# A transformer block on one core: next tile's scores moved one iteration ahead, second norm in other banks, a new order on four engines

## The chip, the cores and the metric

The kernel runs on 1 core of a Trainium2 chip. The metric is the device time of one launch in microseconds: the median of the runs, with their lowest and highest. One execution more is profiled; its rows are the ones read here.

## The reference

128 sequences of 64 tokens and 256 channels go through one transformer block, whose norms take their gain and shift from a condition vector of 64 numbers for each sequence. Everything is float32.

```python
def rmsnorm(x, t, gw, gb, bw, bb):           # gain and shift of each sequence
    g, b = (t @ gw.T + gb)[:, None, :], (t @ bw.T + bb)[:, None, :]
    return g * x * rsqrt(mean(x * x, -1) + 1e-6) + b
def attention(x):                             # 16 heads of 16 channels, 64 x 64 scores
    q, k, v = x @ Wq.T, x @ Wk.T, x @ Wv.T
    return (softmax(q k^T / 4) v) @ Wo.T
def swiglu(x):                                # 1024 hidden channels
    return (silu(x @ gate_w.T) * (x @ hid_w.T)) @ out_w.T
x1  = x + attention(rmsnorm(x, cond, 1))
out = x + x1 + swiglu(rmsnorm(x1, cond, 2))
```

## The kernel before

**Tiles.** A tile is 8 sequences, 512 tokens; there are 16. `iteration(t)` on each engine does the attention of tile t (`attend`), the feed-forward part of tile t-1 (`mlp`; in its names u = t-1), the result of tile t-2 (`finish`) and the first norm and the projections of tile t+1 (`ahead`). Iteration 0 has its own order (`first_tile`), iteration 15 too (`last_tile`); 1 to 14 have the common one, of which 2 to 14 are a loop; 16 and 17 are the common order with parts left out.

**Engines.** Each engine has its own queue, written out by hand in its block, and does it strictly in that order; semaphores join the engines. So a wait at the head of a queue holds up all that stands behind it. TensorE (from L1034) multiplies and transposes into the 8 banks of PSUM: GATE (0), HIDDEN (1), Y and Y+1 (the feed-forward sum), and PAIR to PAIR+3 (attention). ACT (L368), DVE (L674) and GpSimd (L222, written POOL in the rows) work on what comes out. SP (L186) only starts the loads of x and the stores; its order is not touched.

**Precision.** A product of float32 accuracy is made from three passes over operands split in a high and a low part: ACT rounds the high part (`high_norm1`, `high_norm2`, `high_hidden`, `high_attention`, `high_weights`), and GpSimd or DVE subtracts it to have the low part (`low_norm1`, `low_hidden`, `low_weights` on GpSimd; `low_attention` on DVE; of `low_norm2` one channel half on each). Scores, probabilities by values and the transposes are plain float32 products.

**Feed-forward part.** Eight chunks j of 128 hidden channels: `gate(u, j)` and `hid(u, j)`, six products each of 512 columns; ACT `tanh` (L444), DVE `silu` (L786) and `hidden` (L793), ACT `high_hidden` (L449), GpSimd `low_hidden` (L251), then `down(u, j)`, twelve products (L1038 to L1040). `gate(j)` waits for silu(j-1), `hid(j)` for hidden(j-1), since each has one bank.

**Attention.** Two rounds of four pairs of heads. `scores(t, r)` (L1115) fills the four banks PAIR to PAIR+3; for each pair DVE has `row_maxima` (L744) and `shift` (L751), ACT `exp` (L454), DVE `reciprocals` (L758, L763), GpSimd `divide` (L257), TensorE `transpose_probs` (L1123), ACT `keep_transposed` (L459); then `values_probs` (L1139), ACT `first_heads` (L465), DVE `second_heads` (L769), and the high and low part for `project_out`. `scores(t, 1)` waits for second_heads of round 0.

**Norms.** ACT `mean_squares` (L389), GpSimd `inverse_rms` (L231, L234), scaling of the rows (`scale_rows`, DVE L681, four instructions, for the first norm; `scale_second`, ACT L494, and `scale_second_rest`, DVE L688, for the second), eight transposes (`transpose_norm1` L1045, `transpose_norm2` L1054), gain and shift (`first_norm1/2` on DVE, L699 and L706; `second_norm1/2` on ACT, L399, eight instructions), high part (L413, L418), low part (GpSimd L239, L245; DVE L719). The first norm's transposes write GATE and HIDDEN and therefore wait until hidden(5) of the feed-forward part is done (`h_done` 8u+6). The second norm's write PAIR+2 and PAIR+3. `first_residual` (L846) adds the attention to x, `results` (L802) makes the output, `sum_of_inputs` (L280) prepares it. In iteration 0 the splits of the last two weights are made between the pieces of the softmax (`low_weights`, L264).

Of the kernel before, what the change touches and what calls it, by code (L numbers as in the profile page):

```python
# [27 lines left out]
P = 128  # L28
# [25 lines left out]
def conditioned_block(nc, x, condT, modT, attW, gateT, hidT, outT, consts, out):  # L54
# [3 lines left out]
    with ExitStack() as ctx:  # L58
# [164 lines left out]
        def _(pool):  # L223
# [58 lines left out]
            def first_tile(t, attend, mlp, finish, ahead):  # L282
                divide(t, 0)
                inverse_rms(t + 1, ms1, ms1_done, mse1, mse1_done, inv1, inv1_done, scaled1)
# [17 lines left out]
            def last_tile(t, attend, mlp, finish, ahead):  # L302
                sum_of_inputs(t - 1)
                low_hidden(t - 1, 0)
                low_hidden(t - 1, 1)
                divide(t, 0)
                divide(t, 1)
                divide(t, 2)
                divide(t, 3)
                low_hidden(t - 1, 2)  # L310
                low_hidden(t - 1, 3)
                divide(t, 4)
                divide(t, 5)
                low_hidden(t - 1, 4)
                divide(t, 6)
                divide(t, 7)
                low_hidden(t - 1, 5)
                wait(pool, scaled2_rest, t)
                inverse_rms(t, ms2, ms2_done, mse2, mse2_done, inv2, inv2_done, scaled2)
                low_hidden(t - 1, 6)  # L320
                low_hidden(t - 1, 7)
                low_norm2(t)

            def iteration(t, attend, mlp, finish, ahead):
# [10 lines left out]
                if mlp:  # L335
                    low_hidden(t - 1, 1)
                    low_hidden(t - 1, 2)
                if attend:
                    divide(t, 2)
                    divide(t, 3)  # L340
                if mlp:
                    low_hidden(t - 1, 3)
                if ahead:
                    inverse_rms(t + 1, ms1, ms1_done, mse1, mse1_done, inv1, inv1_done, scaled1)
                    low_norm1(t + 1, 0)
                    low_norm1(t + 1, 1)
                if attend:
                    divide(t, 4)
                if mlp:
                    low_hidden(t - 1, 4)  # L350
# [18 lines left out]
        def _(act):  # L369
# [37 lines left out]
            def second_norm2(u):  # L407
                second_norm(u, 2, ps[:, PAIR + 3, :], xT2_done, (xn2_lo_second, u), xn2, xn2_second)
# [94 lines left out]
            def first_tile(t, attend, mlp, finish, ahead):  # L503
                keep_input(t)
                mean_squares(1, x_in, x_loaded, (32, 32), x_scaled1, xT1_done, ms1, ms1_done)
# [3 lines left out]
                exp(t, 2)  # L509
                keep_transposed(t, 1)  # L510
                exp(t, 3)
                high_norm1(t + 1, 0)
                high_weights(2, hid_w_in, 16, hid_w_hi[:, :, :].rearrange("p c n -> p (c n)"), 0)
                keep_transposed(t, 2)
                keep_transposed(t, 3)
                high_weights(3, out_w_in, 16, out_w_hi[:, :, :].rearrange("p j n -> p (j n)"), 1)
                first_heads(t, 0)
                exp(t, 4)
                high_attention(t, 0)
                second_norm1(t + 1, GATE + 1)  # L520
                high_norm1(t + 1, 1)
# [3 lines left out]
                exp(t, 7)  # L525
                keep_transposed(t, 5)
                first_keys(t + 1)
# [7 lines left out]
                first_queries(t + 1)  # L535
# [4 lines left out]
            def last_tile(t, attend, mlp, finish, ahead):  # L540
                tanh(t - 1, 0)
                tanh(t - 1, 1)
                high_hidden(t - 1, 0)
                exp(t, 0)
                keep_input(t)
                exp(t, 1)
                high_hidden(t - 1, 1)
                tanh(t - 1, 2)
                exp(t, 2)
                tanh(t - 1, 3)  # L550
                high_hidden(t - 1, 2)
                keep_transposed(t, 0)
                exp(t, 3)
                keep_transposed(t, 1)
                tanh(t - 1, 4)
                high_hidden(t - 1, 3)
                keep_transposed(t, 2)
                keep_transposed(t, 3)
                first_heads(t, 0)
                exp(t, 4)  # L560
                tanh(t - 1, 5)
                high_hidden(t - 1, 4)
                exp(t, 5)
                exp(t, 6)
                tanh(t - 1, 6)
                exp(t, 7)
                high_attention(t, 0)
                high_hidden(t - 1, 5)
                keep_transposed(t, 4)
                keep_transposed(t, 5)  # L570
                keep_transposed(t, 6)
                keep_transposed(t, 7)
# [4 lines left out]
                high_hidden(t - 1, 6)  # L577
                scale_second(t)
                high_hidden(t - 1, 7)
                high_norm2(t, 0)  # L580
                second_norm2(t)
                high_norm2(t, 1)

            def iteration(t, attend, mlp, finish, ahead):
                if isinstance(t, int) and t == 0:
                    return first_tile(t, attend, mlp, finish, ahead)
                if isinstance(t, int) and t == TILES - 1:
                    return last_tile(t, attend, mlp, finish, ahead)
                if mlp:
                    tanh(t - 1, 0)  # L590
                if attend:
                    exp(t, 0)
                if mlp:
                    high_hidden(t - 1, 0)
                    tanh(t - 1, 1)
                if attend:
                    exp(t, 1)
                    keep_input(t)
                if mlp:
                    tanh(t - 1, 2)  # L600
                if attend:
                    exp(t, 2)
                if mlp:
                    high_hidden(t - 1, 1)
                if attend:
                    keep_transposed(t, 0)
                if mlp:
# [839 lines left out]
```

## Time and profile before

| | us |
|---|---|
| median of 3 runs | 1004.91 |
| lowest and highest | 1001.57, 1005.65 |
| the profiled execution | 1001.78 |
| its span, first to last instruction | 999.8 |
| TensorE busy | 958.1 |
| DVE, ACT, GpSimd busy | 660.1, 561.7, 447.4 |
| mean granted TensorE clock | 0.985 |

The rows of the profile have these forms. A timeline row is: start in us from the span's start, duration, engine, line of the kernel, operation, written tile <- read tiles, shape, how many merged, and in brackets the idle time before it with what ended it. PE is TensorE, PEld its weight loads. Products are pipelined: each row of TensorE is longer than the distance to the next, so the distance between starts is what a product costs (0.23 us for 512 columns), and short waits show only in that distance. Row groups are numbered; the prediction refers to them.

### The profile page before, as it was taken

What the parts mean: (1) busy time and instruction counts of PE and PEld (TensorE: products, weight loads), DVE (VectorE), ACT (ScalarE), POOL (GpSimd) and SP (SyncE); (2) the same over time, 40 slices, a digit from 0 to 9 for tenths busy, and PEclk for the clock granted to TensorE, in tenths of its full rate; (3) what the DMA queues carried; (4) which work ended last, traced back from release to release, by engine and by line L of the source; (5) the groups of instructions that cost most, each with busy time, mean ns of one, the idle gap of its engine ahead of it and who ended that gap; (6) DMA issues with size and microseconds to landing.
All of it is one profiled execution on the core that took longest, in us unless ns stands there. A gap on an engine that the chain in (4) does not pass through costs nothing.

```text
span 999.8 us, 24465 instructions
## 1 busy us (share of the span) xinstructions
PE 958.1 (96%) x9134; PEld 819.7 (82%) x9134; DVE 660.1 (66%) x1178; ACT 561.7 (56%) x1271; POOL 447.4 (45%) x393
## 2 busy tenths in 40 slices
PE   6678999999999999999999999999999999999978
PEld 5467888988888897888889788888978888897767
DVE  3546767676776767677676767767676776766642
ACT  4445656565565656556565655656565565654442
POOL 4443525454452545445254544525454452545242
PEclk9868999999999999999999999999999999999999
DMA  5100000010100001010000101000010100000000
GB/s 168 58 1 22 2 23 22 2 42 0 42 0 21 21 0 42 0 42 0 21 21 0 42 0 42 0 21 21 0 42 0 42 0 21 21 0 22 2 22 22
DMA packets 18971, 21.71 MB, mean 22 GB/s; under 512 B 640, under 2 KB 18240, under 8 KB 18816
## 3 DMA queue, kind: packets, MB, share of 16 engines
q1 hardware_dynamic: 18720, 21.24, 6.4%
q8 instruction: 18, 0.29, 0.1%
q10 hardware_dynamic: 224, 0.10, 0.1%
q14 instruction: 9, 0.07, 0.0%
HBM read 12.95 MB, written 8.39 MB: 21 GB/s over the span
## 4 chain that ended last, share of the span: by engine, by line
PE 89%; ACT 3%; DVE 3%; POOL 2%; issue 2%; DMA 1%; DVEq 0%; ACTq 0%; POOLq 0%
PE ps L1038 10%; PE ps L1040 9%; PE ps L1039 9%; PE ps L1115 6%; PE ps L1150 6%; PE ps L1166 6%; PE ps L1123 6%; PE ps L1158 5%; PE ps L1169 5%; PE ps L1151 5%; PE ps L1167 5%; PE ps L1139 3%; PE ps L1062 3%; PE ps L1065 3%; PE ps L1063 3%
## 5 line engine op out<-in xcount | busy, mean ns | idle before, releaser
L251 POOL TENSOR_TENSOR h_lo<-h,h_hi 128x512 fp32r<-128x512 f32 x128 | 165.2, 1291 | 248.3 <-ACT h_hi L449 248.3
L257 POOL TENSOR_TENSOR probs<-probs,recip 128x512 f32<-128x512 f32 x128 | 132.4, 1045 | 50.5 <-DVE recip L763 50.5
L1038 PE MATMUL ps<-out_w_hi,h_hi 128*128 128x256 f32 x512 | 150.8, 294 | 0.8
L1040 PE MATMUL ps<-out_w_hi,h_lo 128*128 128x256 f32 x512 | 145.0, 283 | 0.0
L1039 PE MATMUL ps<-out_w_lo,h_hi 128*128 128x256 f32 x512 | 144.7, 283 | 0.0
L786 DVE SCALAR_TENSOR_TENSOR shared<-shared,ps 128x512 f32<-128x512 f32 x128 | 87.7, 685 | 77.9 <-ACT shared L444 77.5
L444 ACT ACTIVATE shared<-ps 128x512 f32<-128x512 f32 x128 | 76.7, 600 | 101.5 <-PE ps L1158 100.1
L1150 PE MATMUL ps<-xn_hi,gate_w_hi 128*128 128x512 f32 x256 | 109.5, 428 | 2.3 <-ACT xn_hi L418 1.6
L1166 PE MATMUL ps<-xn_hi,hid_w_hi 128*128 128x512 f32 x256 | 106.1, 414 | 0.9 <-DVE h L793 0.9
L1038 PEld LDWEIGHTS ps<-out_w_hi,h_hi 128*128 128x128 f32 x512 | 97.0, 190 | 11.6 <-POOL h_lo L251 7.2
L459 ACT COPY probsT<-ps 128x512 f32<-128x512 f32 x128 | 73.5, 588 | 50.9 <-PE ps L1123 50.2
L1151 PE MATMUL ps<-xn_hi,gate_w_lo 128*128 128x512 f32 x256 | 101.2, 395 | 0.0
L1167 PE MATMUL ps<-xn_hi,hid_w_lo 128*128 128x512 f32 x256 | 101.0, 395 | 0.0
L793 DVE SCALAR_TENSOR_TENSOR h<-shared,ps 128x512 f32<-128x512 f32 x128 | 87.4, 683 | 18.2 <-PE ps L1169 13.1
L1039 PEld LDWEIGHTS ps<-out_w_lo,h_hi 128*128 128x128 f32 x512 | 97.0, 190 | 1.4
L1040 PEld LDWEIGHTS ps<-out_w_hi,h_lo 128*128 128x128 f32 x512 | 96.8, 189 | 0.0
L744 DVE TENSOR_REDUCE row_max<-ps 128x8 f32<-128x512 f32 x128 | 84.7, 681 | 16.1 <-PE ps L1115 16.1
L449 ACT CAST h_hi<-h 128x512 fp32r<-128x512 f32 x128 | 79.2, 619 | 27.9 <-DVE h L793 27.9
L454 ACT ACTIVATE probs<-probs 128x512 f32<-128x512 f32 x128 | 79.5, 637 | 26.7 <-DVE probs L751 26.7
L758 DVE TENSOR_REDUCE sums<-probs 128x8 f32<-128x512 f32 x128 | 86.2, 673 | 11.9 <-ACT probs L454 11.8
L239 POOL TENSOR_TENSOR xn_lo<-xn,xn_hi 128x512 fp32r<-128x512 f32 x30 | 38.4, 1301 | 117.7 <-ACT xn_hi L413 117.7
L751 DVE TENSOR_TENSOR probs<-ps,row_max 128x512 f32<-128x512 f32 x128 | 87.5, 684 | 1.9
(92 smaller groups left out, 2155.7 us busy)
## 6 DMA issues: line engine op xcount, KB each, us to landing
x_in<-in_x SPq DMA_DIRECT2D x16, 512.0 KB, 3.4
out<-result SPq DMA_DIRECT2D x15, 512.0 KB, 3.0
shared<-in_attT SPq DMA_DIRECT2D x1, 1024.0 KB, 7.5
shared<-in_gateT SPq DMA_DIRECT2D x1, 1024.0 KB, 9.4
shared<-in_hidT SPq DMA_DIRECT2D x1, 1024.0 KB, 4.8
shared<-in_outT SPq DMA_DIRECT2D x1, 1024.0 KB, 5.6
out<-result SPq DMA_DIRECT2D x2, 256.0 KB, 2.2
result<-in_modT SPq DMA_DIRECT2D x1, 256.0 KB, 4.7
```

Source lines behind the costliest of these rows:

```text
L251: nc.gpsimd.tensor_tensor(h_lo[:, j % KEPT, :], h[:, j % 2, :], h_hi[:, j % KEPT, :].bitcast(F32), ALU.subtract).then_inc(h_lo_done, 1)
L257: nc.gpsimd.tensor_tensor(own, own, recip[:, p % TOGETHER, :].unsqueeze(2).to_broadcast([P, SEQS, L]), ALU.mult).then_inc(divided, 1)
L751: nc.vector.tensor_tensor(probs[:, p % TOGETHER, :].rearrange("p (b k) -> p b k", k=L), ps[:, bank_of(p), :].rearrange("p (b k) -> p b k", ...
L786: nc.vector.scalar_tensor_tensor(act_g[:, :], act_g[:, :], 1.0, ps[:, GATE, :], ALU.add, ALU.mult).then_inc(silu_done, 1)
L793: nc.vector.scalar_tensor_tensor(h[:, j % 2, :], act_g[:, :], 0.5, ps[:, HIDDEN, :], ALU.mult, ALU.mult).then_inc(h_done, 1)
L1038: nc.tensor.matmul(dst, a_hi, b_hi, start=first, stop=False, skip_group_check=skip)
L1039: nc.tensor.matmul(dst, a_hi, b_lo, start=False, stop=False, skip_group_check=skip)
L1040: return nc.tensor.matmul(dst, a_lo, b_hi, start=False, stop=last, skip_group_check=skip)
L1150: nc.tensor.matmul(ps[:, GATE, :], gate_w_hi[:, i, w], xn2_hi[:, i, :], start=i == 0, stop=False)
L1151: nc.tensor.matmul(ps[:, GATE, :], gate_w_lo[:, i, w], xn2_hi[:, i, :], start=False, stop=False)
L1166: nc.tensor.matmul(ps[:, HIDDEN, :], hid_w_hi[:, i, w], xn2_hi[:, i, :], start=i == 0, stop=False)
L1167: nc.tensor.matmul(ps[:, HIDDEN, :], hid_w_lo[:, i, w], xn2_hi[:, i, :], start=False, stop=False)
```

## The change

The instructions are the same in kind and number; they are put in another order on TensorE, ACT, DVE and GpSimd, and two banks are changed.

- `scores(t+1, 0)` is issued at the end of iteration t, ahead of the transposes of the second norm, and no longer at the head of iteration t+1. It waits for `first_residual` of tile t (the banks PAIR+2, PAIR+3) and not for the second norm. DVE takes `row_maxima(t+1, 0)` and `shift(t+1, 0)` into iteration t. The scores of tile 0 stand in front of iteration 0.
- `transpose_norm2` writes GATE and HIDDEN (banks 0 and 1), and so waits for all eight hidden chunks of the tile before.
- All four orders are written anew: for the first tile, the last, and the common one.

The diff, cut to the norm, the waits, and the common order of each engine:

```diff
             def second_norm2(u):                                   # ACT
-                second_norm(u, 2, ps[:, PAIR + 3, :], xT2_done, (xn2_lo_second, u), xn2, xn2_second)
+                second_norm(u, 2, ps[:, HIDDEN, :], xT2_done, (xn2_lo_second, u), xn2, xn2_second)
...
             def transpose_norm2(u, c):                             # TensorE
                 pe.wait_ge(scaled2, u + 1)
                 pe.wait_ge(scaled2_rest, u + 1)
-                pe.wait_ge(x1_done, 2 * u + 2)
+                wait(pe, h_done, CHUNKS * u)
...
-                    last = nc.tensor.transpose(ps[:, PAIR + 2 + c, k * P:(k + 1) * P],
+                    last = nc.tensor.transpose(ps[:, GATE + c, k * P:(k + 1) * P],
...
             def scores(t, r):
...
-                    wait(pe, gained2, t)
-                    wait(pe, xn2_second, t)
+                    wait(pe, x1_done, 2 * t)
```

The common order after the change, from the new lines of the diff, conditions left out (t is the tile of attention, u = t-1 of the feed-forward part, n = t+1). What stands in brackets was the order before in the same stretch.

```
GpSimd: low_hidden(u,0) sum_of_inputs(u) divide(t,0) divide(t,1) low_hidden(u,1) divide(t,2)
        low_hidden(u,2) divide(t,3) low_hidden(u,3) inverse_rms(n) low_hidden(u,4) divide(t,4)
        low_norm1(n,0) low_norm1(n,1) divide(t,5) divide(t,6) divide(t,7) low_hidden(u,5) ...
        [... low_hidden(u,3) inverse_rms(n) low_norm1(n,0) low_norm1(n,1) divide(t,4)
        low_hidden(u,4) divide(t,5) ...]
ACT:    exp(t,0) tanh(u,0) exp(t,1) high_hidden(u,0) tanh(u,1) high_hidden(u,1) exp(t,2) tanh(u,2)
        keep_input(t) keep_transposed(t,0) tanh(u,3) high_hidden(u,2) exp(t,3) mean_squares(n)
        tanh(u,4) keep_transposed(t,1) high_hidden(u,3) keep_transposed(t,2) keep_transposed(t,3)
        first_heads(t,0) tanh(u,5) high_hidden(u,4) high_attention(t,0) exp(t,4) second_norm1(n)
        high_norm1(n,0) tanh(u,6) high_norm1(n,1) exp(t,5) keep_transposed(t,4) exp(t,6) exp(t,7)
        high_hidden(u,5) first_keys(n) keep_transposed(t,5) keep_transposed(t,6) first_queries(n)
        keep_transposed(t,7) first_heads(t,1) first_values(n) high_attention(t,1) high_hidden(u,6)
        mean_squares(t) tanh(u,7) scale_second(t) high_hidden(u,7) second_norm2(t) high_norm2(t)
        [... keep_transposed(t,3) tanh(u,5) high_hidden(u,4) first_heads(t,0) second_norm1(n) ...]
DVE:    row_maxima(t,1) low_norm2(u) shift(t,1) results(t-2) silu(u,0) hidden(u,0) row_maxima(t,2)
        row_maxima(t,3) reciprocals(t,0) shift(t,2) silu(u,1) hidden(u,1) reciprocals(t,1)
        silu(u,2) hidden(u,2) reciprocals(t,2) shift(t,3) silu(u,3) hidden(u,3) reciprocals(t,3)
        silu(u,4) hidden(u,4) second_heads(t,0) scale_rows(n) silu(u,5) hidden(u,5)
        row_maxima(t,4) row_maxima(t,5) shift(t,4) first_norm1(n) reciprocals(t,4) ...
        second_heads(t,1) low_attention(t,1) second_queries(n) second_values(n) first_residual(t)
        silu(u,7) hidden(u,7) scale_second_rest(t) row_maxima(n,0) first_norm2(t) shift(n,0)
        [results(t-2) low_norm2(u) row_maxima(t,0) row_maxima(t,1) shift(t,0) silu(u,0) ...
        hidden(u,4) silu(u,5) second_heads(t,0) scale_rows(n) hidden(u,5) row_maxima(t,4)
        row_maxima(t,5) first_norm1(n) shift(t,4) ...]
TensorE: gate hid (u,0) gate hid (u,1) down(u,0) gate hid (u,2) transpose_probs(t,0) gate hid (u,3)
        transpose_probs(t,1) gate hid (u,4) transpose_probs(t,2) transpose_probs(t,3) gate(u,5)
        values_probs(t,0) hid(u,5) scores(t,1) transpose_norm1(n) down(u,1) down(u,2) gate(u,6)
        down(u,3) transpose_probs(t,4) hid(u,6) project_k(n,0) transpose_probs(t,5) project_q(n,0)
        transpose_probs(t,6) project_k(n,1) transpose_probs(t,7) project_v(n,0) values_probs(t,1)
        project_q(n,1) project_v(n,1) down(u,4) project_out(t) gate(u,7) hid(u,7) scores(n,0)
        transpose_norm2(t) down(u,5) down(u,6) down(u,7)
        [scores(t,0) gate hid (u,0) ... transpose_norm1(n) down(u,1) gate(u,6) hid(u,6) down(u,2)
        down(u,3) ... values_probs(t,1) down(u,4) gate(u,7) project_k(n,1) project_out(t)
        project_v(n,1) hid(u,7) down(u,5) transpose_norm2(t) down(u,6) down(u,7)]
```

Of the first tile's order this matters here:

```diff
             def first_tile(t, attend, mlp, finish, ahead):        # GpSimd
...
-                low_weights(3, out_w_lo[:, :, :].rearrange("p j n -> p (j n)"),
-                            out_w_hi[:, :, :].rearrange("p j n -> p (j n)"), 1)
                 low_norm1(t + 1, 0)
+                low_norm1(t + 1, 1)
                 divide(t, 4)
-                low_norm1(t + 1, 1)
                 divide(t, 5)
                 divide(t, 6)
                 divide(t, 7)
+                low_weights(3, out_w_lo[:, :, :].rearrange("p j n -> p (j n)"),
+                            out_w_hi[:, :, :].rearrange("p j n -> p (j n)"), 1)
```

In the same tile ACT does `high_weights(2, ...)` ahead of `mean_squares(1, ...)` instead of behind exp(3). In the last tile GpSimd does low_hidden(14, 6) ahead of the second norm's inverse_rms instead of behind it, ACT does second_norm2 ahead of both high_norm2, and TensorE does gate(14, 7) ahead of the transposes of pairs 5 to 7, hid(14, 7) and project_out(15) directly behind values_probs(15, 1), and down(14, 4) and down(14, 5) behind project_out(15).

## Rows read from the trace of the kernel before

**Rows 1.** The page's busy table: engine, busy us (share of the span), instructions.
```profile
PE 958.1 (96%) x9134; PEld 819.7 (82%) x9134; DVE 660.1 (66%) x1178; ACT 561.7 (56%) x1271; POOL 447.4 (45%) x393
```

**Rows 2.** What TensorE waited for: us in total, times, longest us.
```profile
PE ps L1123 <- POOL probs L257: 10.8, 5, 4.8
...
PE ps L1054 <- ACT shared L494: 4.4, 2, 3.5
...
PE ps L1115 <- ACT shared L399: 2.7, 1, 2.7
```

**Rows 3.** Busy us by engine in two stretches; then granted clock, DMA share, GB/s.
```profile
core 0: us, PE busy (x) PEld busy (x) DVE busy (x) ACT busy (x) POOL busy (x), PEclk, DMA share, GB/s
492.00:551.00 59.00, 58.92 (x585) 50.62 (x586) 40.95 (x74) 35.25 (x82) 26.91 (x24) 1.00 0.06 18
...
900.00:955.00 55.00, 47.59 (x492) 39.62 (x490) 36.70 (x62) 24.72 (x50) 22.42 (x20) 0.98 0.03 11
```

**Rows 4.** Timeline of TensorE, one middle iteration: start us, us, engine, line, operation, tiles.
```profile
492.38 2.02 PE L1115 MATMUL ps<-keys,queries 32*128 32x64 f32 x64
...
502.00 0.39 PE L1150 MATMUL ps<-xn_hi,gate_w_hi 128*128 128x512 f32 x1
...
503.40 0.39 PE L1166 MATMUL ps<-xn_hi,hid_w_hi 128*128 128x512 f32 x1
...
550.61 2.01 PE L1115 MATMUL ps<-keys,queries 32*128 32x64 f32 x64
```

**Rows 5.** Timeline around the end of that iteration, four engines.
```profile
546.75 1.06 PE L1054 MATMUL ps<-consts_sb,shared 128*128 128x128 f32 x8
...
550.32 1.17 ACT L418 CAST xn_hi<-shared 128x512 fp32r<-128x512 f32 x2
...
550.80 1.29 DVE L802 TENSOR_TENSOR result<-ps,x_plus_x 128x512 f32<-128x512 f32 x2 [1.75 <-PE ps L1040]
...
551.05 1.27 POOL L245 TENSOR_TENSOR xn_lo<-shared,xn_hi 128x512 fp32r<-128x512 f32 x1 [2.63 <-ACT xn_hi L418]
...
552.01 0.87 DVE L719 TENSOR_TENSOR xn_lo<-shared,xn_hi 128x512 fp32r<-128x512 f32 x1
...
552.56 0.50 PE L1150 MATMUL ps<-xn_hi,gate_w_hi 128*128 128x512 f32 x1
...
555.62 0.50 PE L1150 MATMUL ps<-xn_hi,gate_w_hi 128*128 128x512 f32 x1
```

**Rows 6.** Timeline between the two rounds of the next iteration, three engines.
```profile
572.08 0.60 ACT L444 ACTIVATE shared<-ps 128x512 f32<-128x512 f32 x1 [0.81 <-PE ps L1158]
...
572.57 0.61 ACT L449 CAST h_hi<-h 128x512 fp32r<-128x512 f32 x1
...
573.18 0.69 ACT L465 ACTIVATE attT_sum<-ps,consts_sb 128x512 f32<-128x512 f32 x1
...
573.90 0.75 DVE L769 SCALAR_TENSOR_TENSOR attT_sum<-ps,consts_sb,attT_sum 128x512 f32<-128x512 f32 x1 [0.51 <-ACT attT_sum L465]
...
574.57 1.13 DVE L681 TENSOR_SCALAR x_scaled<-x_in,inv 128x256 f32<-128x256 f32 x4
...
574.71 2.01 PE L1115 MATMUL ps<-keys,queries 32*128 32x64 f32 x64
...
575.62 0.68 DVE L793 SCALAR_TENSOR_TENSOR h<-shared,ps 128x512 f32<-128x512 f32 x1
...
576.65 1.09 PE L1045 MATMUL ps<-consts_sb,x_scaled 128*128 128x128 f32 x8
```

**Rows 7.** Timeline of DVE's row scaling beside GpSimd, first and last tile.
```profile
36.05 1.04 POOL L257 TENSOR_TENSOR probs<-probs,recip 128x512 f32<-128x512 f32 x1
...
36.11 1.91 DVE L681 TENSOR_SCALAR x_scaled<-x_in,inv 128x256 f32<-128x256 f32 x4 [0.23 <-POOL inv L234]
...
951.57 1.26 POOL L251 TENSOR_TENSOR h_lo<-h,h_hi 128x512 fp32r<-128x512 f32 x1
...
951.63 1.61 DVE L688 TENSOR_SCALAR shared<-shared,inv 128x256 f32<-128x256 f32 x2 [2.42 <-POOL inv L234]
```

**Rows 8.** Timeline of GpSimd in the first tile.
```profile
49.46 4.51 POOL L264 TENSOR_TENSOR out_w_lo<-shared,out_w_hi 128x2048 fp32r<-128x2048 f32 x1
```

More of the change, by code:

```diff
@@ L344, in iteration @@
                     inverse_rms(t + 1, ms1, ms1_done, mse1, mse1_done, inv1, inv1_done, scaled1)
+                if mlp:
+                    low_hidden(t - 1, 4)
+                if attend:
+                    divide(t, 4)
+                if ahead:
                     low_norm1(t + 1, 0)
                     low_norm1(t + 1, 1)
[L347 to L350, printed above, removed]
                 if attend:
@@ L595, in iteration @@
                     tanh(t - 1, 1)
+                    high_hidden(t - 1, 1)
                 if attend:
-                    exp(t, 1)
-                    keep_input(t)
+                    exp(t, 2)
                 if mlp:
@@ L601, in iteration @@
                 if attend:
[L602 to L605, printed above, removed]
+                    keep_input(t)
                     keep_transposed(t, 0)
                 if mlp:
+                    tanh(t - 1, 3)
                     high_hidden(t - 1, 2)
-                    tanh(t - 1, 3)
                 if attend:
@@ L626, in iteration @@
                 if attend:
-                    first_heads(t, 0)
+                    high_attention(t, 0)
+                    exp(t, 4)
                 if ahead:
@@ L827, in _ @@
             second_values(0)
+            row_maxima(0, 0)
+            shift(0, 0)
             def maxima_and_shift(t, p):
@@ L948, in iteration @@
                 if attend:
-                    row_maxima(t, 0)
-                    row_maxima(t, 1)
-                    shift(t, 0)
+                    shift(t, 1)
+                if finish:
+                    results(t - 2)
                 if mlp:
@@ L955, in iteration @@
                 if attend:
-                    shift(t, 1)
+                    row_maxima(t, 2)
+                    row_maxima(t, 3)
                     reciprocals(t, 0)
+                    shift(t, 2)
                 if mlp:
                     silu(t - 1, 1)
+                    hidden(t - 1, 1)
                 if attend:
@@ L1029, in iteration @@
                     scale_second_rest(t)
+                if ahead:
+                    row_maxima(t + 1, 0)
+                if attend:
                     first_norm2(t)
+                if ahead:
+                    shift(t + 1, 0)
             over_tiles(dve, iteration)
@@ L1214, in _ @@
                 project_v(0, half)
+            scores(0, 0)
             def project_out(t):
@@ L1291, in last_tile @@
                 hid(u, 6)
-                down(u, 2)
+                down(u, 3)
+                if ahead:
+                    pe.wait_ge(q_act_done, t + 2)
+                gate(u, 7)
                 transpose_probs(t, 5)
-                down(u, 3)
                 transpose_probs(t, 6)
@@ L1299, in last_tile @@
                 if ahead:
-                    pe.wait_ge(q_act_done, t + 2)
-                gate(u, 7)
+                    pe.wait_ge(q_dve_done, t + 2)
+                hid(u, 7)
+                project_out(t)
                 down(u, 4)
                 down(u, 5)
-                project_out(t)
-                if ahead:
-                    pe.wait_ge(q_dve_done, t + 2)
-                hid(u, 7)
                 for c in range(CH):
@@ L1403, in iteration @@
                     hid(u, 7)
-                    down(u, 5)
+                if ahead:
+                    scores(t + 1, 0)
                 if attend:
```

257 lines of the change are left out of this document (125 added, 132 removed).

## The prediction

> **What bounds the kernel now.** I read the busy table first. TensorE is busy for 958.1 us of a span of 999.8 and no other engine for more than 66% of it, so TensorE bounds the kernel [rows 1]. The list of what TensorE waited for comes next: longest first, three of its twelve entries shown, and none occurs more than five times, so these waits belong to the first and the last tile and not to the middle [rows 2]. In the middle 59 us, TensorE is busy 58.92 at a granted clock of 1.00 [rows 3]. Last the timeline of one middle iteration: scores start at 492.38 and again at 550.61, a period of 58.23 us [rows 4]. Fourteen of the sixteen iterations run this period (t = 1 to 14), so 0.1 us an iteration is 1.4 us of the kernel.
>
> How much of that period could an order give back? A gate or hidden block of six products takes 1.40 us when nothing is in its way (502.00 to 503.40, [rows 4]). With undisturbed lengths read off the same timeline an iteration is 20 such blocks (gate, hidden, queries, keys) of 1.40, 10 of 1.43 (down, values), the output projection 2.84, twice scores 1.94, twice probabilities by values 1.09, and transposes 4.5: 55.7 us. The other 2.5 us are about 0.1 us wherever a block of plain fp32 products hands over to the split ones (0.50 instead of 0.39 for the first product, [rows 4, 5]), which happens 12 times before and 11 times after, 0.1 at the start of each block of scores or of probabilities by values, and waits of 0.1 to 0.2 that the idle column does not show. So the new order can save at most about 0.9 us an iteration, 12 us in all. What it can lose has no such limit: each wait of TensorE in the loop is paid 14 times.
>
> **The loop, part by part.** No product, activation or transfer is added or dropped, so only borders and waits count.
>
> *Scores one iteration early, second norm into the gate banks.* Before, scores and two down blocks stand between the second norm's transposes (546.75) and the gate (552.56), and the transposes wait for the scaled rows. After, gate, hidden and the scores stand behind the output projection, which is 0.4 us more cover for first residual, mean square, power and scaling, so the transposes no longer wait. The gate follows down(7) directly. Behind the transposes come three down blocks, 0.82 + 1.5 + 1.44 + 1.44 = 5.2 us. xn2_hi is complete 4.74 us after the transposes start (550.32 + 1.17 - 546.75, [rows 5]): ready with 0.4 to spare. Together with one hand-over less and small waits gone before hid(6), Tn2 and the seventh probability transpose I count -0.5 us (bounds -0.9 and 0).
>
> *DVE at the start of an iteration.* results (1.29 us, [rows 5]) used to run under the scores, ahead of low_norm2. Now down(7) ends only when the gate begins, and the queue reads row_maxima(1), low_norm2, shift(1), results, silu(0). low_norm2 ends at 5.2 + 0.9 behind the start of the transposes if it must wait for the GpSimd instruction, which it does (below); shift adds 0.6, results 1.25, silu 0.65: gate start + 3.4. gate(1) needs that silu and is ready at gate start + 2.8; it used to start 3.06 after its predecessor (552.56 to 555.62). That is +0.4 of which 0.2 comes back, because down(0) then no longer waits for h_lo: +0.2. The last two products of gate(0) need the low part at +0.93 and get it at about +0.95: +0.1. Bounds for both together 0 and +0.5.
>
> *The step that decides: hidden(5) and the first norm of the next tile.* TensorE may transpose the next tile's rows into GATE and HIDDEN only after hidden(5) (h_done 8u+6). Before, tanh(5) ran at 572.08, silu(5) at 572.71, then second_heads, scale_rows, hidden(5) at 575.62 to 576.30, and the transposes began at 576.65 without waiting [rows 6]. Now ACT does first_heads before tanh(5), and DVE does second_heads, scale_rows, silu(5), hidden(5). Let F be the start of first_heads (573.18 before; it follows the probabilities by values, so it doesn't move). second_heads is F+0.72 to F+1.47, scale_rows F+1.39 to F+2.52 [rows 6]. silu(5) then ends at F+3.15 and hidden(5) at F+3.85. Scores(1) start at F+1.53 and last 1.94, so TensorE is ready at F+3.47: a wait of 0.4 us, new, even if nothing else happens.
>
> *But something else stands there now.* low_hidden(4), 1.29 us on GpSimd, is moved from behind both low_norm1 to directly behind inverse_rms. It waits only for high_hidden(4), which ACT does right behind tanh(5). ACT instructions of this size follow each other every 0.5 us (572.08, 572.57, [rows 6]), so high_hidden(4) ends at F+1.7 and GpSimd starts at F+1.8, in the middle of the four instructions of scale_rows. Twice the trace shows this DVE instruction against a GpSimd one. At 36.11 the four take 1.91 us instead of 1.13, under a GpSimd instruction that ends at 37.09; at 951.63 two take 1.61 instead of half of 1.13, under one that ends at 952.83 [rows 7]. Everywhere else in the loop GpSimd is idle under scale_rows, and there it is 1.13. low_norm2 behaves likewise (at 552.01, 0.87 us and done 0.56 after the GpSimd instruction that began at 551.05, [rows 5]). So DVE loses the rest of the GpSimd instruction. One or two of the four are through when it arrives; the others start about F+3.3 and end at F+3.7; silu(5) ends F+4.35, hidden(5) F+5.05, and the transposes start at F+5.1 instead of F+3.47: a wait of 1.6 us, where the 0.4 stood. Bounds: 0.4 (DVE keeps its place through all four, GpSimd waits) and 1.9 (GpSimd gets in after the first). No row shows a GpSimd instruction that arrives in the middle of such a group, so this is my choice: the two rows say that the one that comes later waits, instruction by instruction. I take 1.6.
>
> The Trainium skill (SBUF — State Buffer, Who interferes with whom) says that DVE instructions such as tensor_scalar in their two-port mode share one port pair with GpSimd, and that the first to issue holds it "for the whole instruction". The two rows agree in size. It speaks of one instruction, so by the rule GpSimd gets in between two of the four and the iteration loses the 1.6; read as a hold over the whole group it would lose 0.4. The same page says that tensor_reduce never contends, and the row maxima and sums would then be free of this in the new order too.
>
> *The rest of the iteration* has to be walked for waits that follow. first_norm1, shift(4), exp(4) and second_norm1 all start behind hidden(5), so they shift with the transposes; xn1_lo is complete about 8.2 us behind them and project_k needs it after down(1), down(2), gate(6), down(3), one transpose and hid(6), 8.6 us. Attention's low part is ready 1.3 us before the output projection. keep_input moves 1.4 us later on ACT, its load lands 3.4 us after issue and mean_squares still finds it. Cost 0, with +0.3 as the upper bound, since three of these margins are under 0.4.
>
> Loop: -0.5 + 0.3 + 1.6 = +1.4 us an iteration, 14 times +19.6 us.
>
> **First tile.** The split of out_w (4.51 us on GpSimd at 49.46) stood before divide(4), and the transposes of probabilities waited 4.8 us for what came behind it ([rows 8] and the first line of [rows 2]). It moves behind divide(7). high_weights(2) moves to where ACT waits for the load of x. divide(4) then follows exp(4), about 3 us earlier. The scores of tile 1 move out from behind the second norm, where TensorE waited 2.7 us and ran them at the lower clock ([rows 2], third line); in their place it waits for the norm uncovered, 4.7 us after the transposes. Net about -1. Sum -4; bounds -7.5 (both waits gone whole) and 0.
>
> **Last tile.** scale_second_rest no longer meets low_hidden(6) (951.63, 1.0 us too long, [rows 7]), and second_norm2 is put before high_norm2(0), but project_out now stands right behind hid(7), with less between it and the last round. -1; bounds -3.5 (the wait for x_scaled2, second line of [rows 2]) and +2.
>
> **Sum.** +19.6 - 4 - 1 = +14.6 us. The profiled execution took 1001.78 us (span 999.8 and 2.0 around it), so 1016.4 by its own time; the median of the three runs shown lies 3.1 us above it, which puts the changed kernel's median at 1019.5; I say 1019. A difference under 0.5%, 5 us, is what I call the same.
>
> **Rivals.** (a) *No collision:* GpSimd comes a little later or waits. Then 0.4 instead of 1.6, loop +0.2, 14 x 0.2 - 5 = -2: 1003. For it: nothing in the trace shows an arrival in mid-group. Against: the two instants hang on the same event F and lie 0.7 us inside the group. Chance 0.17. (b) *The order does what it can:* hidden(5) and silu(0) are both in time, and the small savings hold: -0.5 x 14 - 5 = -12: 993. For it: TensorE's list shows no wait in the loop now, so the queues have slack. Against: it needs SBUF work and first_heads shorter by 0.4 us than they have been in all 15 tiles. Chance 0.17. (c) *The scores change nothing* since TensorE is full anyway; that is contained in (a). (d) *Clock:* 1.6 us of waiting each iteration lowers the granted clock and all that follows runs slower, over 1030. Against: the last tile's stretch of 55 us has 7.4 us without TensorE work in it and a mean clock of 0.98 ([rows 3], second line). Chance 0.05. The forecast (collision, +1.0 to +1.8 an iteration) has 0.61; its own range is 1010 to 1027.
>
> The range takes in (a): 1001 to 1027. Faster 0.18, same 0.17, slower 0.65.
>
> **What would show it.** In the changed profile: TensorE's list has a wait for DVE's h (L793) before the first norm's transposes, 14 times, 1.3 to 1.7 us each; scale_rows lasts 2.3 us instead of 1.13 with low_hidden inside it; period 59.6; gate(1) starts 3.4 us behind gate(0); no wait before the second norm's transposes; divide(4) of tile 0 near 53. If scale_rows stays at 1.13 and the period is near 58.4, the collision was wrong and the rest stands. If the period is under 58, the placement of first_heads was harmless and I misread the chain behind F.

## The result, and the profile after

The changed kernel takes 1028.79 us (median of four runs, 1027.54 to 1029.90), the kernel before 1003.71 in the same comparison (1001.57 to 1005.65). The ratio is 1.025, interval 1.0223 to 1.0277: 25 us slower. The forecast was 1019, slower, between 1001 and 1027. The direction came true; the time lies 10 us above the forecast and 2 us outside the range. The profiled execution took 1028.87 us, with a span of 1026.8 (before: 999.8).

The page of the changed kernel: busy time of each engine, the granted clock of TensorE in 40 slices, and the chain of work that ended last, by engine. The first line answers to [rows 1].

```profile
PE 964.8 (94%) x9134; PEld 827.9 (81%) x9134; DVE 684.9 (67%) x1178; ACT 561.4 (55%) x1271; POOL 456.9 (44%) x393
...
PEclk9989999999999999999999999999999999999999
...
PE 82%; DVE 10%; issue 3%; ACT 2%; POOL 1%; DMA 1%; DVEq 0%; SPq 0%; ACTq 0%; POOLq 0%
```

TensorE is busy 6.7 us longer than before, yet no product was added; the span grew by 27.0. The slices of 25 us hide the clock: all read 9 in the middle, although the mean granted clock of the execution fell from 0.985 to 0.973.

What TensorE waited for (total us, times, longest), to be held against [rows 2]:

```profile
PE ps L1046 <- DVE h L796: 20.1, 14, 1.4
PE ps L1125 <- POOL probs L257: 9.4, 5, 5.0
...
PE ps L1152 <- ACT xn_hi L421: 4.5, 2, 3.7
...
PE ps L1152 <- DVE shared L789: 2.9, 14, 0.3
```

Before, no wait occurred more than five times. Now the first norm's transposes (L1046) wait for DVE's product h 14 times, 20.1 us in all, once in each full iteration: this is the step on which the forecast rested. The fourth line is gate(1) waiting 0.2 us for silu(0).

The same instant in a middle iteration, after; it answers to [rows 6]. Columns: start, duration, engine, line, operation, and in brackets the idle time before it and what ended that.

```profile
587.54 0.69 ACT L468 ACTIVATE attT_sum<-ps,consts_sb 128x512 f32<-128x512 f32 x1 [1.86 <-PE ps L1141]
588.13 0.59 ACT L447 ACTIVATE shared<-ps 128x512 f32<-128x512 f32 x1
588.26 0.75 DVE L772 SCALAR_TENSOR_TENSOR attT_sum<-ps,consts_sb,attT_sum 128x512 f32<-128x512 f32 x1 [3.25 <-ACT attT_sum L468]
588.60 0.62 ACT L452 CAST h_hi<-h 128x512 fp32r<-128x512 f32 x1
588.93 2.15 DVE L684 TENSOR_SCALAR x_scaled<-x_in,inv 128x256 f32<-128x256 f32 x4
589.07 2.01 PE L1117 MATMUL ps<-keys,queries 32*128 32x64 f32 x64
...
589.30 1.36 POOL L251 TENSOR_TENSOR h_lo<-h,h_hi 128x512 fp32r<-128x512 f32 x1 [2.03 <-ACT h_hi L452]
591.00 0.67 DVE L789 SCALAR_TENSOR_TENSOR shared<-shared,ps 128x512 f32<-128x512 f32 x1
591.71 0.69 DVE L796 SCALAR_TENSOR_TENSOR h<-shared,ps 128x512 f32<-128x512 f32 x1
```

With F = 587.54, the start of first_heads: scale_rows starts at F+1.39 as forecast, GpSimd's low_hidden(4) starts at F+1.76 inside it, and the four DVE instructions take 2.15 us where they took 1.13. silu(5) and hidden(5) follow, and TensorE's transposes start at F+4.98 (forecast: F+5.1):

```profile
592.52 1.65 PE L1046 MATMUL ps<-consts_sb,x_scaled 128*128 128x128 f32 x8 [1.44 <-DVE h L796]
```

So far the forecast holds to 0.2 us. What it left out stands in the windows (busy us and instructions of each engine, then the granted clock), of the loop and of three stretches of this iteration:

```profile
100.00:900.00 800.00, 777.08 (x7548) 670.26 (x7547) 560.19 (x965) 452.81 (x1040) 361.52 (x316) 0.98 0.05 17
589.00:592.80 3.80, 2.36 (x68) 2.16 (x68) 3.77 (x8) 0.74 (x2) 1.36 (x1) 1.00 0.00 0
592.80:596.20 3.40, 3.40 (x19) 3.40 (x18) 3.25 (x6) 1.98 (x6) 0.00 (x0) 0.51 0.00 0
596.40:650.00 53.60, 53.38 (x486) 45.51 (x484) 35.25 (x62) 31.40 (x72) 26.18 (x23) 1.00 0.06 20
```

After the wait the granted clock is 0.51 for 3.4 us, 1.2 GHz of 2.4, and then full again ("clock stretch" below). The products show it too: one of the down block takes 0.41 us in that stretch and 0.28 behind it.

```profile
594.40 0.41 PE L1041 MATMUL ps<-out_w_hi,h_lo 128*128 128x256 f32 x1
...
597.04 0.28 PE L1041 MATMUL ps<-out_w_hi,h_lo 128*128 128x256 f32 x1
```

Such a stretch follows the wait in 11 of the 14 iterations (all but t = 2, 7 and 11). Before, the loop had none.

**Where the 27.0 us are.** I cut both executions at the start of the second gate block of iterations 1 and 15. Before:

```profile
89.90 0.40 PE L1150 MATMUL ps<-xn_hi,gate_w_hi 128*128 128x512 f32 x1
...
905.25 0.50 PE L1150 MATMUL ps<-xn_hi,gate_w_hi 128*128 128x512 f32 x1
```

and after:

```profile
85.42 0.47 PE L1152 MATMUL ps<-xn_hi,gate_w_hi 128*128 128x512 f32 x1
...
934.62 0.50 PE L1152 MATMUL ps<-xn_hi,gate_w_hi 128*128 128x512 f32 x1
```

The start is 4.5 us shorter. The 14 periods between take 849.2 instead of 815.35, +33.85 (60.66 each instead of 58.24). The rest, to the end of the span (the tail), takes 92.2 instead of 94.55, -2.35. Sum +27.0. Of the loop, the three iterations without a clock stretch have periods of 59.45 to 59.48, that is +1.22 an iteration or +17 us; the other eleven have about 61.0, 1.5 more each, which is the remaining 17 us.

### The profile page after: what moved, and what is told of

Same layout as the page of the kernel before. It is cut to its first block, busy times and chain, and to the rows that moved or that the text cites. A ratio compares the mean times of both kernels' runs of the same rounds, so it can differ in the third digit from the quotient of the medians.

```text
span 1026.8 us, 24437 instructions
## 1 busy us (share of the span) xinstructions
PE 964.8 (94%) x9134; PEld 827.9 (81%) x9134; DVE 684.9 (67%) x1178; ACT 561.4 (55%) x1271; POOL 456.9 (44%) x393
## 4 chain that ended last, share of the span: by engine, by line
PE 82%; DVE 10%; issue 3%; ACT 2%; POOL 1%; DMA 1%; DVEq 0%; SPq 0%; ACTq 0%; POOLq 0%
PE ps L1039 9%; PE ps L1041 9%; PE ps L1040 9%; PE ps L1152 6%; PE ps L1125 5%; PE ps L1168 5%; PE ps L1160 5%; PE ps L1171 5%; PE ps L1169 5%; PE ps L1153 5%; PE ps L1141 3%; PE ps L1117 3%; PE ps L1065 3%; DVE x_scaled L684 3%; PE ps L1066 3%; PE ps L1068 3%
## 5 line engine op out<-in xcount | busy, mean ns | idle before, releaser
L251 POOL TENSOR_TENSOR h_lo<-h,h_hi 128x512 fp32r<-128x512 f32 x128 | 169.1, 1322 | 241.7 <-ACT h_hi L452 239.8
L257 POOL TENSOR_TENSOR probs<-probs,recip 128x512 f32<-128x512 f32 x128 | 135.0, 1065 | 136.7 <-DVE recip L766 136.7
L1039 PE MATMUL ps<-out_w_hi,h_hi 128*128 128x256 f32 x512 | 154.6, 302 | 0.0
L1041 PE MATMUL ps<-out_w_hi,h_lo 128*128 128x256 f32 x512 | 149.3, 292 | 0.0
L1040 PE MATMUL ps<-out_w_lo,h_hi 128*128 128x256 f32 x512 | 149.2, 291 | 0.0
L1152 PE MATMUL ps<-xn_hi,gate_w_hi 128*128 128x512 f32 x256 | 107.0, 418 | 7.5 <-ACT xn_hi L421 4.5
L1039 PEld LDWEIGHTS ps<-out_w_hi,h_hi 128*128 128x128 f32 x512 | 103.0, 201 | 6.6 <-POOL h_lo L251 5.7
L1040 PEld LDWEIGHTS ps<-out_w_lo,h_hi 128*128 128x128 f32 x512 | 102.4, 200 | 0.8
L1041 PEld LDWEIGHTS ps<-out_w_hi,h_lo 128*128 128x128 f32 x512 | 101.8, 199 | 0.0
L1125 PE MATMUL ps<-consts_sb,probs 128*128 128x128 f32 x512 | 75.2, 275 | 9.5 <-POOL probs L257 9.4
```

Of the source, the lines that this page charges most:

```text
L251: nc.gpsimd.tensor_tensor(h_lo[:, j % KEPT, :], h[:, j % 2, :], h_hi[:, j % KEPT, :].bitcast(F32), ALU.subtract).then_inc(h_lo_done, 1)
L257: nc.gpsimd.tensor_tensor(own, own, recip[:, p % TOGETHER, :].unsqueeze(2).to_broadcast([P, SEQS, L]), ALU.mult).then_inc(divided, 1)
L1039: nc.tensor.matmul(dst, a_hi, b_hi, start=first, stop=False, skip_group_check=skip)
L1040: nc.tensor.matmul(dst, a_hi, b_lo, start=False, stop=False, skip_group_check=skip)
L1041: return nc.tensor.matmul(dst, a_lo, b_hi, start=False, stop=last, skip_group_check=skip)
L1125: last = nc.tensor.transpose(ps[:, bank_of(p), k * P:(k + 1) * P], probs[:, p % TOGETHER, k * P:(k + 1) * P], ident)
```

## The experiments

The theory after the result: the mishap is one wait, made of 0.4 us of order and 1.0 us of collision; it costs itself and, in most iterations, a stretch at half clock that costs as much again. The rivals: the collision is not what makes scale_rows long; the clock falls for another reason than this wait; the moves named in the change cost by themselves. "Period" below is the mean of the 14 periods cut as above; times are medians, and each ratio is against the kernel before on the same chip.

**1. The collision taken away** (GpSimd's queue of the changed kernel):

```
-                if mlp:
-                    low_hidden(t - 1, 4)
                 if attend:
                     divide(t, 4)
                 if ahead:
                     low_norm1(t + 1, 0)
                     low_norm1(t + 1, 1)
+                if mlp:
+                    low_hidden(t - 1, 4)
```

> The changed kernel with one line moved: in the common order GpSimd does low_hidden(4) behind both low_norm1 again, so that it is idle while DVE scales the rows. Theory (collision, then wait, then clock): scale_rows falls from 2.15 to 1.13 us, TensorE's wait before the first norm's transposes from 1.4 to 0.3-0.4, the half-clock stretches of 3.4 us behind that wait (11 of 14 iterations) are gone, the period is near 58.4. Time 1028.8 - 14 x 1.0 - 11 x 1.6 = 997, within 3. Rival (the clock falls because of the new order as a whole, not because of this wait): only the wait shortens, 1028.8 - 14 = 1014. Second rival (first_heads ahead of tanh(5) is what costs, not GpSimd): over 1020.

Measured: 1004.86 us, ratio 1.002 (1.0004 to 1.0036), 24 us less than the changed kernel. Its timeline has scale_rows short and the wait at the forecast remainder of 0.4:

```profile
573.69 1.13 DVE L684 TENSOR_SCALAR x_scaled<-x_in,inv 128x256 f32<-128x256 f32 x4
...
576.27 1.09 PE L1046 MATMUL ps<-consts_sb,x_scaled 128*128 128x128 f32 x8 [0.43 <-DVE h L796]
```

No clock stretch is left in the loop. The time is 8 us above the 997 expected. Most of that is the period, 58.82 and not 58.4: low_hidden(4) now holds up divide(5), so the transposes of probabilities behind the first block of keys wait too (from the start of that block to theirs it is 1.71 us instead of 1.40, and the wait on probs counts 15 times instead of 5). A queue that is relieved at one place is loaded at another. The last tile also has 6.8 us at half clock here, and the tail is 2.8 us longer than that of the changed kernel (95.0).

**2. The wait filled, the collision kept**: six products with zero weights, added into a bank that is being accumulated.

```
                     if mlp:
+                        for n in range(6):
+                            nc.tensor.matmul(ps[:, Y, :], zeros[:, :], att_w_hi[...],
+                                             start=False, stop=False, ...)
                         pe.wait_ge(h_done, CHUNKS * u + 6)
```

> The changed kernel with six more products of 512 columns, weights zero, accumulated into the feed-forward bank behind scores(t,1), where TensorE would wait for hidden(5): 6 x 0.23 = 1.4 us of work in the place of the wait; nothing else changes. Theory: DVE and GpSimd still collide (scale_rows 2.15) and the transposes start no earlier, but TensorE is not idle and its clock stays: period 59.5 in all iterations, 1028.8 - 11 x 1.6 = 1011. Rival (clock drops have nothing to do with the wait): 1029 or a little more.

Measured: 1014.04 us (1010.00 to 1016.35), ratio 1.0122 (1.0084 to 1.0161), 3 us above the expectation. The loop, and DVE's scaling (count, then shortest, median and longest ns of one):

```profile
100.00:900.00 800.00, 797.23 (x7797) 683.26 (x7797) 571.54 (x984) 463.60 (x1058) 369.84 (x322) 1.00 0.05 17
```
```profile
L687 DVE TENSOR_SCALAR x_scaled<-x_in,inv x64: 340/346/1361, 9.9 to 877.6; 128x256 f32<-128x256 f32 x64
```

The collision is there (1361 ns for the instruction that is caught), TensorE is late by the same time, but it is busy instead of waiting: no clock stretch in the loop, and a period of 59.46, the one of the undisturbed iterations of the changed kernel. 14 x (60.66 - 59.46) = 16.8 us is therefore the price of the lowered clock, and idleness ahead of the transposes is what lowers it in this loop.

**3. The chain around F put right, GpSimd's order kept**: ScalarE does tanh(5) and high_hidden(4) before first_heads, VectorE silu(5) before second_heads.

```
-                    first_heads(t, 0)
                 if mlp:
                     tanh(t - 1, 5)
                     high_hidden(t - 1, 4)
                 if attend:
+                    first_heads(t, 0)
                     high_attention(t, 0)
...
                     hidden(t - 1, 4)
+                    silu(t - 1, 5)
...
                     scale_rows(t + 1, x_in, inv1, ...)
                 if mlp:
-                    silu(t - 1, 5)
                     hidden(t - 1, 5)
```

> The changed kernel with two moves in the common order: ACT does tanh(5) and high_hidden(4) ahead of first_heads(0) again, DVE silu(5) ahead of second_heads(0) again; GpSimd's order stays as changed, so low_hidden(4) now starts before scale_rows and is nearly over when that begins. Theory: hidden(5) is done before TensorE has finished scores(1); no wait, no clock drop, period 57.8 to 58.1. Time 1028.8 - 14 x 1.5 - 11 x 1.6 = 990, within 4. Rival (clock falls with the order as a whole): 1028.8 - 20 = 1008.

Measured: 991.94 us (989.21 to 992.28), ratio 0.9891 (0.9866 to 0.9916): 37 us under the changed kernel and 11 under the one before, the best version of all. Its timeline:

```profile
567.18 0.69 DVE L789 SCALAR_TENSOR_TENSOR shared<-shared,ps 128x512 f32<-128x512 f32 x1 [2.15 <-ACT shared L447]
...
567.73 1.30 POOL L251 TENSOR_TENSOR h_lo<-h,h_hi 128x512 fp32r<-128x512 f32 x1 [0.44 <-ACT h_hi L452]
...
569.04 1.13 DVE L684 TENSOR_SCALAR x_scaled<-x_in,inv 128x256 f32<-128x256 f32 x4
...
570.09 0.68 DVE L796 SCALAR_TENSOR_TENSOR h<-shared,ps 128x512 f32<-128x512 f32 x1
571.12 0.53 PEld L1046 LDWEIGHTS ps<-consts_sb,x_scaled 128*128 128x128 f32 x5
```

low_hidden(4) ends at 569.03 and scale_rows begins at 569.04: the two no longer overlap. hidden(5) ends 0.35 us before the transposes, so nothing waits for it. Period 57.96, and 92.2 us of tail.

**4. A longer wait without the collision**: experiment 1 with two reductions of 0.6 us over a constant tile between scale_rows and silu(5).

```
                     scale_rows(t + 1, x_in, inv1, ...)
+                    for n in range(2):
+                        nc.vector.tensor_reduce(unused[:, n, :], att_w_hi[...], AX_X, ALU.max)
```

> The first experiment (low_hidden(4) out of the way) with two DVE reductions of 0.6 us over a constant tile put between scale_rows and silu(5): the wait of TensorE is made again, 0.4 + 1.2 = 1.6 us, but without any meeting of DVE and GpSimd. Theory: scale_rows stays at 1.13, the half-clock stretches come back in most iterations, time 1028 to 1033. Rival (it is the shared access of DVE and GpSimd that slows things, not the length of the wait): 997 to 1014.

Measured: 1041.03 us, ratio 1.0396 (1.0373 to 1.0419), 8 us above the upper end of the expectation.

```profile
596.14 1.13 DVE L685 TENSOR_SCALAR x_scaled<-x_in,inv 128x256 f32<-128x256 f32 x4
597.19 1.27 DVE L988 TENSOR_REDUCE unused<-att_w_hi 128x8 f32<-128x512 f32 x2
...
599.90 0.54 PE L1051 MATMUL ps<-consts_sb,x_scaled 128*128 128x128 f32 x3 [1.61 <-DVE h L797]
```
```profile
600.40:603.80 3.40, 3.40 (x19) 3.40 (x18) 3.22 (x7) 2.20 (x7) 0.00 (x0) 0.51 0.00 0
```

With scale_rows undisturbed the wait of 1.61 us alone lowers the clock, and in all 14 iterations. The period is 61.40: 58.82 of experiment 1, 1.2 more of wait, and 1.4 of clock. I had counted on fewer stretches.

**5. Half that delay** (one reduction):

> The fourth experiment with one DVE reduction of 0.6 us instead of two: a wait of about 1.0 us before the first norm's transposes, without GpSimd. So far 0.4 us left the clock alone, 1.4 lowered it in 11 of 14 iterations, 1.6 in all. If the length of the wait decides and 1.0 is short enough: no half-clock stretch, 1004.9 + 14 x 0.6 = 1013. If any wait near 1 us is enough: all 14, 1035. I expect the first or a few drops, 1013 to 1020.

Measured: 1014.63 us, ratio 1.0114 (1.0082 to 1.0147). The wait is 1.0 us in every iteration; two of the fourteen have a clock stretch (periods 60.9, the others 59.1 to 59.3). Stretches by length of the wait, then: 0.4 us none in 14 (experiment 1), 1.0 two, 1.44 eleven, 1.61 fourteen.

The length does not decide alone. Iterations 2, 7 and 11 of the changed kernel had the same 1.44 us as the others and kept a full clock, and in experiment 4 all periods are alike, so its fourteen say less than fourteen different cases would. The last tile shows it too. In every trace TensorE waits 1.58 us there, ahead of the scores of the second round and not ahead of transposes. The changed kernel has a full clock around it (scores at 955.26), experiment 1 has half the clock for 6.8 us just behind the same wait (scores at 928.47):

```profile
951.00:960.00 9.00, 7.42 (x153) 6.29 (x152) 4.07 (x7) 3.00 (x6) 2.13 (x2) 1.00 0.01 2
...
929.60:936.40 6.80, 6.80 (x51) 6.10 (x48) 4.52 (x8) 1.66 (x3) 1.70 (x2) 0.50 0.01 2
```

Experiments 2, 5 and 6 have 3.4 us at half clock behind this wait, experiments 8 and 9 have 6.8, and the kernel before and experiments 3, 4 and 7 have none. What chooses between them stays open.

**6. Another block as cover**: down(1) goes ahead of the first norm's transposes, as cover for hidden(5).

```
                     scores(t, 1)
+                if mlp:
+                    down(u, 1)
                 if ahead:
...
                 if mlp:
-                    down(u, 1)
                     down(u, 2)
```

> The changed kernel with down(1) issued ahead of the first norm's transposes instead of behind them: 1.44 us of work that was already there goes into the wait of 1.4 us. Theory: the wait for hidden(5) and the clock drops are gone, but the chain from these transposes to the low part of the norm has 1.4 us less in front of project_k, which begins to wait by 0.5 to 1.1 us; period 58.5 to 59.1, time 995 to 1008. Rival (a filled wait is a saved wait): period 58.0, time 991.

Measured: 1006.63 us, ratio 1.0036 (1.0018 to 1.0053). The wait for h is gone and no clock stretch is in the loop, but the block is missing where it stood:

```profile
PE ps L1065 <- POOL xn_lo L239: 9.2, 14, 0.7
```

The keys now wait up to 0.7 us for the norm's low part. Period 59.01. Taking 1.44 us of cover away leaves a wait of 0.66, so the margin ahead of project_k was about 0.8 us, twice the 0.4 that the prediction named.

**7. The named moves alone**: to the kernel before, only the scores ahead, the gate banks for the second norm, down(5) behind its transposes, and VectorE's new head of the iteration.

```
-                if finish:
-                    results(t - 2)
+                if attend:
+                    row_maxima(t, 1)
                 if mlp:
                     low_norm2(t - 1)
...
+                if ahead:
+                    row_maxima(t + 1, 0)
                 if attend:
                     first_norm2(t)
+                if ahead:
+                    shift(t + 1, 0)
...
-                    last = nc.tensor.transpose(ps[:, PAIR + 2 + c, k * P:(k + 1) * P],
+                    last = nc.tensor.transpose(ps[:, GATE + c, k * P:(k + 1) * P],
```

> The kernel before with only the named moves: scores of the next tile ahead of the second norm's transposes, down(5) behind them, these transposes into the GATE and HIDDEN banks, and DVE's first five items of an iteration as the changed kernel has them. ACT's and GpSimd's orders and everything from hidden(0) to the last project_v stay as before. Theory: TensorE was full, so the scores' early start is worth only border effects: period 58.0 to 58.4 where it was 58.24, no clock drop in the loop, time within 5 us of the kernel before (1003). Rival (the moves are what gains, the rest of the new order only loses): 990 to 995. Second rival (the moves themselves bring the loss): over 1010.

Measured: 1007.58 us, ratio 1.0039 (1.0023 to 1.0054). The period is 58.32 against 58.24. What the change is named after is worth nothing in the loop, +0.1. It costs 5.0 us once, at the end of tile 0: the scores no longer stand behind the second norm's transposes, so TensorE waits for the norm uncovered, ahead of the first gate block, which starts 4.5 us later than before (85.14):

```profile
89.62 0.76 PE L1155 MATMUL ps<-xn_hi,gate_w_hi 128*128 128x512 f32 x1 [3.68 <-ACT xn_hi L418]
```

In the last tile its transposes of the second norm wait 4.1 us where they waited 3.5, and the tail stays at 94.6.

**8 and 9. Two tries for more, on top of experiment 3**: results later in VectorE's queue, behind hidden(0),

```
                 if attend:
                     shift(t, 1)
-                if finish:
-                    results(t - 2)
                 if mlp:
                     silu(t - 1, 0)
                     hidden(t - 1, 0)
+                if finish:
+                    results(t - 2)
```

> The third experiment (tanh(5) and silu(5) early, 991.9 us) with results(t-2) put behind hidden(0) on DVE instead of ahead of silu(0). Theory: gate(1) no longer waits 0.2 to 0.3 us for silu(0) in 14 iterations, of which up to 0.2 comes back as down(0)'s wait for h_lo: -0.1 to -0.3 an iteration, 988 to 990. Rival (DVE's order there costs nothing): 992.

and the same with row_maxima(2), row_maxima(3) and shift(2) behind hidden(1) as well.

> The third experiment (991.9 us) with DVE's head of the iteration in the order silu(0), hidden(0), results(t-2), reciprocals(0), silu(1), hidden(1), and row_maxima(2), row_maxima(3), shift(2) behind these. The sixth experiment lost because three softmax items stood between results and silu(1), so that gate(2) waited 0.7 us. Theory: gate(1) begins 0.3 us earlier, down(0) gives 0.2 of it back, gate(2) does not wait; period 57.7 to 57.9, 988 to 990. Rival (the maxima pushed back now delay the softmax and a later step of TensorE): period 58.2 or more, 995.

Both missed. The first took 1004.10 us (ratio 1.0011, 0.9998 to 1.0024), 12 more than experiment 3. In experiment 3 results fills the time before silu(0); now VectorE is idle there for 0.92 us, and results delays all between hidden(0) and silu(1), for which gate(2) waits:

```profile
561.31 0.50 PE L1152 MATMUL ps<-xn_hi,gate_w_hi 128*128 128x512 f32 x1 [0.72 <-DVE shared L789]
```

This wait of 0.7 us comes in nearly every iteration and lowers no clock; the period is 58.81. The second took 996.31 (0.9944, 0.9927 to 0.9961), with a period of 58.14 instead of 57.96: gate(3) now starts 0.25 us later against the block before it, since silu(2) stands behind the softmax items that were pushed back:

```profile
556.28 0.69 DVE L789 SCALAR_TENSOR_TENSOR shared<-shared,ps 128x512 f32<-128x512 f32 x1 [0.35 <-ACT shared L447]
...
557.02 0.19 PEld L1152 LDWEIGHTS ps<-xn_hi,gate_w_hi 128*128 128x128 f32 x1 [0.24 <-DVE shared L789]
```

Each has the 6.8 us at half clock in its last tile, 95.0 us of tail instead of 92.2.

## Why the prediction was right in direction and wrong in size

- **"The step that decides"**: right. It forecast 14 waits of 1.3 to 1.7 us for h; there are 14 of 1.44. Experiments 1 and 3 take the collision away in two different ways and the wait shrinks to 0.43 or goes.
- **"Something else stands there now"**: right in the choice between its bounds. GpSimd does get in between two of the four, as the Trainium skill's rule of one instruction (SBUF — State Buffer, Who interferes with whom) has it; the group takes 2.15 us, where 2.3 was forecast, and the three that are not caught stay at 0.34 to 0.35.
- **-0.5 for borders and small waits, +0.3 for VectorE's head**: their sum, -0.2, is what the undisturbed period leaves: 59.46 - 58.24 - 1.44 = -0.2. The parts were not measured one by one, except that scores, banks and head together give +0.1 in experiment 7. gate(1) starts 3.41 us behind gate(0), forecast 3.4, by these rows of the changed kernel:

```profile
627.85 0.39 PE L1152 MATMUL ps<-xn_hi,gate_w_hi 128*128 128x512 f32 x1
...
631.26 0.50 PE L1152 MATMUL ps<-xn_hi,gate_w_hi 128*128 128x512 f32 x1 [0.20 <-DVE shared L789]
```

- **First tile, -4**: -4.5. divide(4) starts at 53.29 as forecast, but the transposes still wait 5.0 us for it ([rows 2]: 4.8). Experiment 7 loses 5.0 us here with the scores moved and the old order of the queues, so it seems to be the other reordering that gives the time back; no run has that alone.
- **Last tile, -1**: -2.35, inside its bounds, in part by luck. All experiments but the seventh keep this last tile's order, and their tails are 92.1 to 92.2 us without half clock in the middle of it, 93.2 to 93.4 with 3.4 us at half clock and 95.0 with 6.8.
- **The step that failed: "Clock ... Chance 0.05"**, and with it the sum of the loop, which held no term for it. By its other terms the loop would have been +17 (forecast 19.6) and the whole about 1012; the clock adds 16 to 17. The argument against it, the last tile's mean clock of 0.98 over a stretch with 7.4 us of idleness [rows 3], was a misreading: 0.98 of 55 us already holds about 2 us at half clock, and a mean over 55 us says nothing about what one wait does. The rival itself said "over 1030", that is more than this case brought; a price of 1.5 us for some of the waits would have been the fitting one, and the upper end of the range with it. The trace of the kernel before has such a stretch, 3.4 us long; it begins inside those 55 us, near the end of the 3.5 us wait for the second norm ([rows 2], second line). This window shows it (the granted clock is the third number from the right):

```profile
952.80:956.20 3.40, 2.85 (x14) 2.88 (x15) 2.73 (x5) 0.62 (x1) 1.31 (x2) 0.51 0.02 5
```

- **+3.1 us for the median**: not there. The median of the changed kernel, 1028.79, is that of its profiled execution, 1028.87. Without this term the forecast would have been 1016; by the profiled executions it gave +14.6 where 27.0 was measured, and only this term brought the stated time within 10 us.

## What to carry to other kernels

Where TensorE is full, price a new wait in a loop at its length, and if it comes near a microsecond or above, add the slower products behind it: here 1.44 us of wait cost 1.22 net by itself and as much again by the clock. A wait that cannot be removed is cheaper filled here (1014.04 against 1028.79), though the repair of the queue order that made it is worth more (991.94). When a queue is reordered, write down for each instruction who waits for it and by how many tenths, since of the six reorderings in experiments 1, 3 and 6 to 9 only the third did not move a wait to another place.

## What was not expected of the hardware

- A single idle stretch of TensorE lowered the granted clock to 0.51 for 3.4 us and cost about 1.5 us beside itself: never with 0.4 us of waiting, nor with 0.7 at two other places of the loop, in 2 of 14 iterations with 1.0, in 11 with 1.44, in all 14 with 1.61. The same instant with products of zero weights in the wait's place kept 1.00. Why 3 of the 14 were spared at 1.44 is open, and why the 1.58 us of the last tile were followed by half the clock in six traces and not in the other five; so is what part the small products of the scores just ahead of the wait have in it. The Trainium skill (TensorE: Matmul & The Clock Gate, A second HAM failure mode: psum-queue depth-cycling) tells of short idleness between groups of products that makes the clock swing between its two levels; the traces agree that idleness of this size can do it, and here one wait of 1.44 us in a period of 60 is enough.
- The scores that stand before such a wait had a granted clock of 1.00; only what comes after it is slow. The list of waits alone shows 20.1 us of the 33.85 that the 14 periods gained; the rest hides in TensorE's busy time, which grows from 958.1 to 964.8.
